# A routed block of linear attention and experts: rows, bias and outputs of the first tiles put into another order on VectorE, TensorE and ScalarE

## What is computed

```
def _L0_attn_ref(x, wq, bq, wk, bk, wv, bv, wo, bo):
    q = _fm((x @ wq + bq).reshape(B, N, H, Dh))        # _fm is elu + 1
    k = _fm((x @ wk + bk).reshape(B, N, H, Dh))
    v = (x @ wv + bv).reshape(B, N, H, Dh)
    kv = jnp.einsum('bnhd,bnhe->bhde', k, v)
    z = 1.0 / (jnp.einsum('bnhd,bhd->bnh', q, k.sum(axis=1)) + 1e-06)
    scores = jnp.einsum('bnhd,bhde,bnh->bnhe', q, kv, z)
    return scores.reshape(B, N, D) @ wo + bo
...
    expert_idx = jnp.argmax(router_probs, axis=-1)
    p_max = jnp.max(router_probs, axis=-1, keepdims=True)
    def expert_mlp(w1, bb1, w2, bb2):
        h = jax.nn.gelu(x @ w1 + bb1, approximate=False)
        return h @ w2 + bb2
...
    x = x + _L0_attn_ref(_layernorm(x, axis=-1), ...)
    x = x + _L0_ffn_ref(_layernorm(x, axis=-1), ...)
```

## Time and profile before

| | us |
|---|---|
| median of 3 runs | 103.03 |
| lowest and highest | 103.0, 103.6 |
| the profiled execution, device time | 103.47 |
| its span, first to last instruction | 101.7 |
| its granted TensorE clock, mean | 0.989 of 2.4 GHz |
| TensorE matmul busy | 89.3 (88% of the span) |
| VectorE busy | 72.4 (71%) |
| ScalarE, GpSimd busy | 56.1, 55.8 (55% each) |

### The profile page before, as it was taken

One profiled execution on the slowest core, in us unless ns is written; L12 is line 12 of the kernel. 1 busy time (PEld: TensorE's weight loads), 2 busy tenths in 40 slices (PEclk: granted clock), 3 DMA queues, 4 the chain that ended last, 5 costly groups with the idle time before them and its releaser, 6 DMA issues.

```text
span 101.7 us, 2570 instructions
## 1 busy us (share of the span) xinstructions
PE 89.3 (88%) x700; PEld 77.3 (76%) x700; DVE 72.4 (71%) x318; ACT 56.1 (55%) x177; POOL 55.8 (55%) x96
## 2 busy tenths in 40 slices
PE   4999999999989969999899479999999999999600
PEld 1267878978975868463899369999999999999500
DVE  4869966389779898959789799667767667753400
ACT  3153986656703552656677256676675775776200
POOL 6544828903187488775167627563553553553650
PEclk9999999999999999999999999999999999999995
DMA  2999999990000101125202355534101000010000
GB/s 47 347 343 336 373 300 291 333 256 9 0 27 27 53 27 36 53 62 128 52 27 65 100 113 124 128 105 120 55 29 52 16 10 17 19 32 22 0 0 0
DMA packets 12125, 10.52 MB, mean 103 GB/s; under 512 B 1472, under 2 KB 9920, under 8 KB 12112
## 3 DMA queue, kind: packets, MB, share of 16 engines
q1 hardware_dynamic: 10576, 7.82, 28.5%
q0 software_dynamic: 1248, 2.14, 6.3%
q10 hardware_dynamic: 288, 0.40, 1.2%
HBM read 7.68 MB, written 3.13 MB: 106 GB/s over the span
## 4 chain that ended last, share of the span: by engine, by line
PE 64%; DVE 13%; issue 7%; DMA 5%; POOL 3%; ACT 2%; POOLq 2%; DVEq 1%; SPq 0%
PE psum L1273 17%; PE psum L1257 16%; PE psum L1187 5%; PE psum L1060 4%; PE psum L1102 4%; DMA routed_rows<-rows,slot_at 3%; PE psum L1137 3%; POOL routed_rows L397 2%; PE psum L1243 2%; DVE sc L694 2%; PE psum L1119 2%; PE psum L1128 2%; DMA slot<-routed_rows 2%; PE psum L1080 2%; DVE zed L690 2%
## 5 line engine op out<-in xcount | busy, mean ns | idle before, releaser
L404 POOL DMA_INDIRECT out_dram<-slot x23 | 22.4, 973 | 19.5 <-DVE slot L953 17.6
L586 ACT ACTIVATE hid<-psum,b_sb 128x128 f32<-128x128 f32 x92 | 26.3, 369 | 11.2 <-PE psum L1257 11.0
L1257 PE MATMUL psum<-tT,w_st 128*128 128x128 f32 x184 | 24.4, 275 | 0.0
L1273 PE MATMUL psum<-w_sb,hid 128*128 x184 | 24.3, 276 | 0.0
L1273 PEld LDWEIGHTS psum<-w_sb,hid 128*128 128x128 f32 x184 | 22.3, 192 | 0.2
L1257 PEld LDWEIGHTS psum<-tT,w_st 128*128 128x128 f32 x184 | 22.4, 192 | 0.0
L397 POOL DMA_INDIRECT routed_rows<-rows,slot_at x16 | 16.0, 1000 | 11.2 <-DVE rows L768 3.5
L953 DVE SCALAR_TENSOR_TENSOR slot<-psum,slot 128x128 f32<-128x128 f32 x23 | 8.1, 351 | 11.6 <-PE psum L1273 11.2
L1187 PE MATMUL psum<-ones_bf 128*128 128x512 bf16 x39 | 11.9, 450 | 1.5 <-DVE ones_bf L612 1.5
L921 DVE COPY w_st<-w_sb 128x512 f32 x20 | 8.8, 444 | 1.8 <-issue 1.2
L1187 PEld LDWEIGHTS psum<-ones_bf 128*128 128x128 bf16 x39 | 4.3, 112 | 5.7 <-issue 1.9
(11 more groups left out here) (194 smaller groups left out, 150.9 us busy)
## 6 DMA issues: line engine op xcount, KB each, us to landing
w_sb<-in_W_dram SPq DMA_DIRECT2D x2, 1024.0 KB, 7.9
w_sb<-in_W_dram SPq DMA_DIRECT2D x4, 512.0 KB, 10.0
slot<-routed_rows SPq DMA_DIRECT2D x23, 66.0 KB, 2.1
x_sb<-in_x_dram SPq DMA_DIRECT2D x3, 256.0 KB, 4.1
routed_rows<-pad_rows SPq DMA_DIRECT2D x1, 528.0 KB, 5.8
b_sb<-in_b_dram SPq DMA_DIRECT2D x1, 512.0 KB, 7.2
out_dram<-slot POOLq DMA_INDIRECT x23
w_sb<-in_wcat_dram ACTq DMA_DIRECT2D x1, 264.5 KB, 3.7
```

Of the source, the lines that this page charges most:

```text
L404: pool.indirect_dma_start(out=out_flat, out_offset=bass.IndirectOffsetOnAxis(ap=slot[:, i, NUMBER:NUMBER + 1].bitcast(U32), axis=0), in_=s ...
L586: act.activation(hid[:, i % 2, c, :], src[:, c * P:(c + 1) * P], ACT.Gelu, bias=b1_sb[:, bass.ds(expert[i] * FC + c, 1)]).then_inc(hid_s, 1)
L1257: last = pe.matmul(dst[:, c * P:(c + 1) * P], w1_st[:, i % W1_RING, c * P:(c + 1) * P], tT[:, i % RING, :], start=True, stop=True)
L1273: last = pe.matmul(y_ps[i % 2][:, 0:D], hid[:, i % 2, c, :], w2_sb[c][:].rearrange("p e d -> p (e d)")[:, bass.ds(expert[i] * D, D)], star ...
```

## The change

Four things are moved or added.

1. Before the loop over tiles, TensorE transposes tile 1 ahead of the four warming products and the last `rank_sums`, not behind them. ScalarE copies tile 1's transpose ahead of the tanh of the last batch. The rows of tile 2 go from ScalarE to VectorE (HB_ACT = 2), ahead of `last_slots_and_probability`.
2. Tiles 5 and 6 get an expert table of their own, `expert_c`, taken from `start_c`, with a semaphore `middle_expert`, and a small comparison `past_c` of 46 elements for the short cut. The large `past_b` moves behind it. The groups of four values begin with tile 7.
3. VectorE's rows, outputs and bias of the first tiles are put between the steps of the table. For tiles 1 and 2 the output comes first and the bias after it; the scatter of a tile's output therefore waits for `xb_s` too.
4. TensorE's order around tile 5 becomes H(4), D(3), T(5), D(4), T(6), H(5), H(6), T(7), D(5); ScalarE copies 5 and 6 one behind the other ahead of `gelu(5)`. T(2) comes behind H(1) too.

```diff
-    HB_ACT = 3
+    HB_ACT = 2
...
         def late_values(engine, i):
             g = i - EARLY
+            if g == 0:
+                return tile_values(engine, expert_c, E - 1)
             return tile_values(engine, expert_b, E - 1, slice(g, min(g + GROUP, LATE)))
 
+        def slots_order(i):
+            if i == EARLY - 2:
+                return ()
+            if i == EARLY - 1:
+                return (i + 1, i + 2)
+            return (i + 2,) if i + 2 < SLOT_TILES else ()
+
         def late_group(i):
-            return EARLY <= i < SLOT_TILES and (i - EARLY) % GROUP == 0
+            g = i - EARLY - MIDDLE
+            return i == EARLY or 0 <= g < LATE - MIDDLE and g % GROUP == 0
...
             def scatter_output(i):
                 pool.wait_ge(y_s, i + 1)
+                pool.wait_ge(xb_s, i + 1)
...
             copy_tT(0)
+            copy_tT(1)
             act.wait_ge(lms_s, B - 1)
             act.activation(ex[:, tiles(B - 1), :], lms[:, tiles(B - 1), :], ACT.Tanh, scale=0.5).then_inc(ex_s, 1)
-            copy_tT(1)
-            normal_rows(2)
...
             scaled_logits(B - 1)
+            normal_rows(HB_ACT)
             last_slots_and_probability()
...
-            for i in range(HB_ACT, EARLY):
-                normal_rows(i)
+            normal_rows(HB_ACT + 1)
...
+            late_step(dve.tensor_tensor(past_c[:], tile_no[:, 0:MIDDLE, 0:SB - 1],
+                                        incl_b[:, 0:SB - 1].unsqueeze(1).broadcast_to([P, MIDDLE, SB - 1]), ALU.is_ge))
+            normal_rows(HB_ACT + 2)
             late(8)
...
             output_rows(0)
+            dve.wait_ge(middle_start, 1)
+            dve.tensor_scalar(expert_c[:], start_c[:], REGION_SHIFT, E - 1, ALU.logical_shift_right,
+                              ALU.bitwise_and).then_inc(middle_expert, 1)
+            late_step(dve.tensor_tensor(past_b[:], tile_no[:, :, 0:SB - 1],
+                                        incl_b[:, 0:SB - 1].unsqueeze(1).broadcast_to([P, LATE, SB - 1]), ALU.is_ge))
+            output_rows(1, biased=False)
+            late(12)
             late_step(dve.tensor_tensor(stepped_b[:], past_b[:].unsqueeze(1).broadcast_to([P, 2, LATE, SB - 1]),
                                         step_b[:].unsqueeze(2).broadcast_to([P, 2, LATE, SB - 1]), ALU.mult))
-            late(12)
+            output_rows(2, biased=False)
+            late(13)
             late_step(dve.tensor_reduce(stepped_n[:], stepped_b[:], AX_X, ALU.add))
-            add_bias(1)
-            late(13)
+            normal_rows(EARLY)
+            late(14)
...
+            add_bias(1, biased=False)
...
-            output_rows(1)
+            dve.wait_ge(middle_expert, 1)
+            expert += late_values(mybir.EngineType.DVE, EARLY)
+            for i in range(EARLY, EARLY + MIDDLE):
+                stage_w1(i)
+            normal_rows(EARLY + 1)
             dve.wait_ge(late_start, 1)
             late_step(dve.tensor_tensor(again[:], start_b[:], start_own[:], ALU.subtract))
...
+            add_bias(2, biased=False)
             for i in range(SLOT_TILES):
-                if i >= 2:
+                if i >= 3:
                     output_rows(i)
...
             slots_T(0)
+            slots_T(1)
             keep_warm(WARM_LAST[4], warm2_ps)
             rank_sums(B - 1)
-            slots_T(1)
             hidden(0)
...
-                late_rows = i + 2 in (EARLY, EARLY + 1)
-                if i + 2 < SLOT_TILES and not late_rows:
-                    slots_T(i + 2)
+                rows_late = i in (0, EARLY)
...
+                if i == EARLY - 1:
+                    slots_T(EARLY)
+                    down(i)
+                    slots_T(EARLY + 1)
```

More of the change, by code:

```diff
@@ L175, in preln_linear_attention_moe @@
         stepped_b = sb("stepped_b", [P, 2, LATE, len(BEHIND) * E - 1])
+        past_c = sb("past_c", [P, MIDDLE, len(BEHIND) * E - 1])
+        expert_c = sb("expert_c", [P, MIDDLE], I32)
         stepped_c = sb("stepped_c", [P, MIDDLE, len(BEHIND) * E - 1])
@@ L599, in _ @@
             for i in range(SLOT_TILES):
-                if i + 2 < SLOT_TILES:
-                    copy_tT(i + 2)
+                for t in slots_order(i):
+                    copy_tT(t)
                 if i + 1 == EARLY:
+                    act.wait_ge(middle_expert, 1)
+                if i + 1 == EARLY + MIDDLE:
                     act.wait_ge(late_expert, 1)
@@ L922, in stage_w1, with normal_rows @@
                                 w1_sb[:].rearrange("p e f -> p (e f)")[:, bass.ds(expert[i] * F, F)]).then_inc(w1_s, 1)
+            def normal_rows(i):
+                dve.wait_ge(slot_in[i], 16)
+                if i >= H_RING:
+                    dve.wait_ge(tT_mm, i - H_RING + 1)
+                dve.tensor_scalar(hb[:, i % H_RING, :], slot[:, i, xs], slot[:, i, SCALE:SCALE + 1],
+                                  slot[:, i, SHIFTED:SHIFTED + 1], ALU.mult, ALU.add).then_inc(h_s, 1)
             dve.wait_ge(w1_in, 32)
@@ L932, in _, with add_bias @@
             scaled_logits(B - 1)
+            normal_rows(HB_ACT)
             last_slots_and_probability()
[L935 to L942, removed]
+            def add_bias(i, biased=True):
+                if not biased:
+                    dve.wait_ge(y_s, i + 1)
                 dve.scalar_tensor_tensor(out=slot[:, i, xs], in0=b2_sb[:, bass.ds(expert[i] * D, D)],
@@ L976, in _ @@
             late_step(dve.tensor_tensor(step_b[:, 1, :], cnt_b_ps[:, SB + 1:2 * SB], count_b[:, 0:SB - 1], ALU.subtract))
-            late(5)
-            late_step(dve.tensor_tensor(past_b[:], tile_no[:, :, 0:SB - 1],
-                                        incl_b[:, 0:SB - 1].unsqueeze(1).broadcast_to([P, LATE, SB - 1]), ALU.is_ge))
             late(6)
@@ L1278, in _ @@
             slots_T(0)
+            slots_T(1)
             keep_warm(WARM_LAST[4], warm2_ps)
             rank_sums(B - 1)
-            slots_T(1)
             hidden(0)
             for i in range(SLOT_TILES):
-                late_rows = i + 2 in (EARLY, EARLY + 1)
-                if i + 2 < SLOT_TILES and not late_rows:
-                    slots_T(i + 2)
+                rows_late = i in (0, EARLY)
+                if not rows_late and EARLY - 1 != i:
+                    for t in slots_order(i):
+                        slots_T(t)
+                if i == EARLY - 1:
+                    slots_T(EARLY)
+                    down(i)
+                    slots_T(EARLY + 1)
                 if i + 1 < SLOT_TILES:
                     hidden(i + 1)
-                if late_rows:
+                if rows_late:
                     slots_T(i + 2)
+                if i == EARLY - 1:
+                    continue
                 if i == EARLY:
+                    pe.wait_ge(middle_expert, 1)
+                if i == EARLY + MIDDLE:
                     pe.wait_ge(late_expert, 1)
```

30 lines of the change are left out of this document (15 added, 15 removed).

## The result

The changed kernel takes 104.87 us in the median of 4 runs (103.82 to 105.69), the kernel before beside it 103.31 (103.0 to 104.49). The ratio is 1.0095, with an interval of [1.0057, 1.0133]. In both kernels some executions take about 1.5 us more at a lower granted clock; the ratios leave most of these out, the medians don't.

What follows compares the result with a forecast made beforehand. TensorE, never without work from tile 7 on, was taken as the bound: T(8) at 63.5 instead of 64.28, 0.8 less with the tail unchanged, takes 103.47 to 102.7 profiled, 102.2 against the median of 103.03; range 101.5 to 103.0.

Steps and rivals of the forecast that it cites:

- T(5): TensorE's transpose of tile 5, before at 59.20: forecast at 57.66 by VectorE's rows, no longer late.
- D(4): TensorE's W2 product of tile 4: forecast to wait for ScalarE's gelu until 58.28, TensorE standing for 0.7.
- D(5): TensorE's W2 product of tile 5: at 62.35 at the earliest, 2.58 behind the start of its W1 product.
- rows of tile 6: VectorE's rows for tile 6's transpose: forecast at 59.2, behind a load of values and two copies.
- T(8): TensorE's transpose of tile 8: forecast at 63.5 instead of 64.28, 0.8 less, passed on to the end.
- The start: TensorE ahead of the loop over tiles: ranks 0.05 later, tile 0's W1 product begins near 49.14.
- VectorE's wait for D(2): VectorE ahead of the output of tile 2: a new wait of 0.6 for TensorE's W2 product of that tile.
- the order around tile 6: TensorE's new order there: tile 6's transpose at 59.66, late by 0.5, tile 5's W1 product at 59.77.
- The bias of tile 2, load and copy 0.45: VectorE ahead of the rows of tile 7: these steps take 0.45, with the copy at 60.45.
- VectorE is slower than reckoned: Rival: VectorE's loads 0.72 each, rounds 1.53, tile 8's transpose near 64.2; 102.5 to 103.0, chance 0.22.
- The reads of tiles 7 and 8: Rival: SyncE's read of tile 7 starts 1.2 later, may land at 62.2; late reads or ranks 103.0 to 103.6, chance 0.10.
- The sum behind T(8): From tile 8's transpose on: tail unchanged, VectorE 0.5 late to tile 5's output but rows of tile 9 by 64.8.

Runs made afterwards that it cites:

- the version with both edits: Changed kernel with two unused columns ahead of the table of late experts and TensorE's load of the last late expert moved ahead of tile 7's transpose: 103.15, 0.9977.
- the old groups and TensorE's load moved: Changed kernel with tiles 5 to 8's experts loaded at once, aligned, and no TensorE load between tile 7's transpose and tile 5's W2 product: 102.5 against 103.27, 0.9965.
- Two versions: Changed kernel with late experts loaded in aligned fours and TensorE's load moved: 102.5; the same with the change's first part undone: 102.48.

## Why the prediction was wrong

The forecast was 102.2 with a range of 101.5 to 103.0; the time was above the range, on the other side of the kernel before. Its steps, each against H(0) (49.14 forecast, 49.35 in the trace), with the version with both edits (49.00) and that with the old groups and TensorE's load moved (48.80) as the last numbers:

| step | forecast | changed | both edits | old groups, moved |
|---|---|---|---|---|
| T(5) | 8.52 | 8.69 | 8.69 | 8.72 |
| D(4), which waits for ScalarE | 9.14 | 9.15 | 9.15 | 9.15 |
| rows of tile 6 | 10.06 | 10.16 | 10.14 | 10.29 |
| T(6) | 10.52 | 10.62 | 10.60 | 10.75 |
| copy of tile 7's W1 | 11.31 | 12.34 | 11.68 | 11.47 |
| rows of tile 7 | 12.46 | 13.40 | 12.74 | 12.52 |
| D(5) | 13.21 | 14.72 | 13.65 | 13.44 |
| rows of tile 8 | 13.86 | 14.70 | 14.18 | 13.83 |
| T(8) | 14.36 | 15.61 | 14.82 | 14.33 |

- *The start, VectorE's wait for D(2), the order around tile 6:* right to 0.1 to 0.2. VectorE stood 0.62 ahead of the output of tile 2 where 0.6 was forecast, T(5) came 0.33 behind the end of D(3), forecast at 0.18, and D(4) waited for ScalarE.
- *"The bias of tile 2, load and copy 0.45":* the step that failed. It measured 1.27. The price was read from loads of aligned groups, and I took the group's length as the same since it still holds four values. The row that spoke against it, SyncE's loads of `start_b` at 0.88 for the same count, was in the trace, and it was read past. With an aligned load it is 0.62 to 0.67, so the term was also 0.2 short in itself: it leaned on the 0.34 of the row at 62.81, where most of a load is covered by the operations under way, and only one was under way here.
- *TensorE's load of values:* missing from the sum. The change moves it from behind H(6) to between T(7) and D(5), and D(5) was reckoned from gelu(5) alone. It makes 0.87 from T(7) to D(5) where 0.25 do without it. By gelu(5) alone, which ended at 62.53, D(5) could have begun near 62.7, 13.3 behind H(0), as forecast (13.21); it began at 64.07, behind T(7) and the load.
- *Rivals:* "VectorE is slower than reckoned" named the open loads, at 0.72 each, and so ended at 103.0, still under the truth: the mechanism was right, its size was not. The reads of tiles 7 and 8 landed in 1.8 to 2.1 and limited nothing. The rows of tile 7 took 0.34 at 62.75, and those of tile 8 0.59; why rows of one shape differ was not tested.
- *The sum behind T(8):* right, 37.42 and 37.44.

With the two causes away and nothing else changed, T(8) comes 14.82 behind H(0), 0.46 later than forecast, and the kernel takes 103.15, still above the range. Of the 0.46, 0.37 are there at the copy of tile 7's W1. Two versions do reach the forecast for T(8) (14.33 and 14.37) and take 102.5 against 102.2, but they have one load fewer on VectorE ahead of tile 7, which the forecast had counted, and their T(5) and rows of tile 6 are 0.2 later than forecast: their agreement with 14.36 is luck.

## What to carry to other kernels

When an edit regroups what an engine loads into registers, look at the byte where each group starts, not only at how many values it has: two columns of padding decided between 0.34 and 1.05 us here. What a load costs depends on the work that is in flight on its engine: nearly its whole length behind one short operation (1.00 of 1.08 on VectorE, 0.62 for 0.56 behind a lone transpose on TensorE), and nothing that could be seen in the last stretch, where TensorE is never without work. So put it behind such work, and count it for each engine whose order the change touches. Where two rows of one kind differ by more than twice for the same count, find out why before using either as a price.

## What the runs showed of the hardware

- A load of four values into registers: 0.34 on VectorE, 0.31 on ScalarE, 0.33 on TensorE from a 16-byte boundary; 1.05, 0.93 and 1.00 from 8 bytes off it. That the group's start alone does this is shown in both directions, by the padding in the kernel before and in the changed one. Only these two starts were tried.
- Two values take longer than four aligned ones: `expert_c` takes 0.68 on VectorE, 0.57 on ScalarE and 0.56 on TensorE in the changed kernel.
- On two chips TensorE's work was seen by the other engines up to 4.7 us after its end as the profile has it (D(1), begun at 55.29 and 1.06 long, released VectorE at 61.0), and VectorE and ScalarE were then released within 0.05. The kernel before took 3 to 4.5% more there than on the other chips, and the changed one 7% more. What holds the signals up, and why the changed kernel loses more, is open: neither the alignment of the loads, nor their grouping, nor the place of TensorE's load made a difference that could be measured there, and the first part of the change was not undone there.
